# A decoder kernel on one core: order of the attention step, and the product for the values

## The reference

```
h = layernorm(x)
q, k, v = h @ Wq, src @ Wk, src @ Wv        # src is h or the context
p = softmax(scale * q k^T + mask)           # per sequence and head, 64 x 64
x = x + (p v) @ Wo
```

## Time and profile before

| | us |
|---|---|
| median of 3 runs (lowest, highest) | 4896.48 (4889.78, 4901.68) |
| the profiled execution, its own time | 4900.09 |
| its span in the profile | 4898.2 |
| mean granted TensorE clock | 0.889 |
| busy: PE, DVE, POOL, ACT | 4007.7, 3203.4, 2994.6, 2059.5 |

### The profile page before, as it was taken

How to read it: one execution, slowest core, us unless ns; L and a number is a source line. 1 busy time by engine, 2 the same in 40 slices (tenths; PEclk the granted TensorE clock), 3 DMA queues, 4 the chain that set the end, 5 groups by cost and what they waited for, 6 DMA issues and landing times. The chain is left out here.

```text
span 4898.2 us, 215645 instructions
## 1 busy us (share of the span) xinstructions
PE 4007.7 (82%) x85067; PEld 2918.6 (60%) x85076; DVE 3203.4 (65%) x10848; ACT 2059.5 (42%) x5737; POOL 2994.6 (61%) x4949
## 2 busy tenths in 40 slices
PE   8999977254899978656999997559879998889988
PEld 6777754132566666523777774335547776667766
DVE  5875668422344688787556874753337878888866
ACT  4555545011344444365555554112225543336632
POOL 6766632276455699688556762038876777777710
PEclk9999988555899998755999997879998999999999
DMA  3000012433100022200000002113431000000000
GB/s 94 5 13 19 19 28 57 78 62 54 37 0 0 18 39 39 35 1 1 2 0 15 22 18 54 42 46 75 77 62 35 0 15 16 16 9 1 0 13 24
DMA packets 380509, 139.58 MB, mean 28 GB/s; under 512 B 216487, under 2 KB 373239, under 8 KB 380055
## 3 DMA queue, kind: packets, MB, share of 16 engines
q1 hardware_dynamic: 345430, 107.60, 9.3%
q0 software_dynamic: 34816, 28.34, 4.0%
HBM read 91.46 MB, written 43.85 MB: 28 GB/s over the span
## 5 line engine op out<-in xcount | busy, mean ns | idle before, releaser
L1051 DVE TENSOR_REDUCE rowmax<-ps 128x16 f32<-128x1024 f32 x512 | 626.3, 1223 | 488.0 <-PE ps L678 487.7
L696 PE MATMUL ps<-prob,kT 32*64 32x256 f32 x9216 | 781.7, 408 | 8.7 <-issue 2.4
L721 PE MATMUL ps<-v,probT 64*64 64x64 f32 x36864 | 764.6, 227 | 5.3 <-issue 2.2
L721 PEld LDWEIGHTS ps<-v,probT 64*64 64x64 f32 x36864 | 683.8, 140 | 57.4 <-issue 16.0
L678 PE MATMUL ps<-kblock,qT 32*64 32x256 f32 x8192 | 697.0, 410 | 17.2 <-DVE rowmax L1060 14.2
L900 ACT ACTIVATE probT<-ps 128x1024 f32<-128x1024 f32 x512 | 518.0, 1012 | 353.4 <-PE ps L708 353.0
L585 POOL TENSOR_TENSOR kblock<-kT,key_scale 128x512 f32<-128x512 f32 x576 | 599.8, 1041 | 18.2 <-ACT kT L878 7.6
L587 POOL TENSOR_TENSOR prob<-qT,key_scale 128x512 f32<-128x512 f32 x576 | 601.5, 1044 | 0.0
L561 POOL TENSOR_TENSOR vareps<-moments,eps 128x1 f32<-128x1 f32 x522 | 98.8, 189 | 745.7 <-DVE negmean L1025 745.6
L887 ACT ACTIVATE xn<-x_res,nmr,rstd 128x128 f32 (+1 forms) x512 | 252.7, 494 | 513.6 <-POOL nmr L567 349.5
L708 PEld LDWEIGHTS ps<-mT,pick_bf 32*64 32x64 bf16 x16384 | 311.7, 108 | 221.2 <-ACT mT L857 74.1
(11 more groups left out here) (380 smaller groups left out, 9655.7 us busy)
## 6 DMA issues: line engine op xcount, KB each, us to landing
ctxT<-in_ctxT SPq DMA_DIRECT2D x256, 64.0 KB, 1.8
held<-in_g_w SPq DMA_DIRECT2D x16, 836.0 KB
ctxT<-in_ctxT SPq DMA_DIRECT2D x256, 32.0 KB, 1.9
table<-prob SPq DMA_DIRECT2D x32, 256.0 KB, 2.4
x_dram<-x_res SPq DMA_DIRECT2D x32, 256.0 KB, 2.4
x_res<-x_dram SPq DMA_DIRECT2D x16, 512.0 KB, 6.9
x_res<-in_x SPq DMA_DIRECT2D x8, 512.0 KB, 7.5
x_res<-in_e_w SPq DMA_DIRECT2D x64, 64.0 KB
```

The costliest lines, as they stand in the source:

```text
L696: mm = nc.tensor.matmul(out.rearrange("p (h s) -> p h s", h=GH), k.kT[rows, buf, S * b:S * b + S], k.qblock[rows, buf, :, S * b:S * b + S] ...
L721: mm = nc.tensor.matmul(k.ps_o[S * b:S * b + S, u, S * hh:S * hh + S], k.probT[rows, buf, at:at + S], k.v9[rows, buf, (HD + 1) * h:(HD + 1 ...
L1051: nc.vector.tensor_reduce(spread, heads, AX.X, ALU.max).then_inc(soft.did["max_raw"], 1)
```

## The change

PE's step now begins with queries, keys and the two transposes; then stand all the waits; then the output product, the values and the transpose of the output of it-7; then the added rows and the scores; and the mixing is last. Within the scores the maxima are subtracted first (the small products open the sum in PSUM) and the key scores are added. The values are one product of 128 columns, except in L1_xattn, which keeps two; the exchange of the halves for the last eight heads is made in the copy out of PSUM, in three instructions (all partitions and the first eight heads, and twice half the partitions and the last eight). `xnT` loses its second copy and ACT the instruction that made it (L866, and L860 in L3_ffn). ACT copies the group of `front_psum` first, then that of `yv_psum`. DVE finds the maxima first and takes the reciprocal and the normalized output last. In L3_xattn the values were one product already and their copy stays one instruction.

```diff
+WHOLE = (slice(0, P), slice(0, HEADS), slice(0, P))
+def value_parts():
+    first, second, low, high = slice(0, HEADS // 2), slice(HEADS // 2, HEADS), slice(0, S), slice(S, P)
+    return [(slice(0, P), first, slice(0, P)), (low, second, high), (high, second, low)]
...
@@ attention_pe, step
-        if value is not None or turn is not None or out is not None:
-            (the waits and products of this group)
...
+        if mixes is not None:
+            after(pe, c, "v_done", it, mb)
         after(pe, c, "kT_done", it, 3)
...
         if norm is not None:
             after(pe, c, "xn_done", it, 1)
             mm = nc.tensor.transpose(k.ps_xT, k.xn[:, b1, :], k.ident)
         if less is not None:
-            values_mixable(mixes, it, mb)
-            if early:
-                scores_writable(score1, score2, it)
             after(pe, c, "max_done", it, 5)
             mm = nc.tensor.matmul(k.ps_mT, top_halves(k.rowmax[:, b5, :]), k.ident_bf[:, :], start=True, stop=True)
         if mm is not None:
             mm.then_inc(c.front_psum, 1)
+        mm = None
+        if score1 is not None:
+            after(pe, c, "max_done", it, 4)
+            after(pe, c, "kblock_done", it, 3)
+        if score2 is not None:
+            after(pe, c, scores_read(c, it, 6), it, 6)
+            after(pe, c, "qblock_done", it, 5)
         if mixes is not None:
-            for hh in range(HEADS // 2):
-                mm = mix(mixes, (par - mb) % NB, hh)
-            mm.then_inc(mixes.did["o_psum"], 1)
+            after(pe, c, "exp_done", it, mb)
+        if value is not None or turn is not None or out is not None:
+            after(pe, c, values_read(c, it, 4), it, 4)
+            after(pe, c, "y_read", it, 9)
+            after(pe, c, "oT_done", it, 8)
+        if out is not None:
+            mm = nc.tensor.matmul(k.ps_y, k.oT[:, b8, :], weights(out, 3), start=True, stop=True)
+        if mixes is not None and turn is None:
+            after(pe, c, "on_done", it, mb + 1)
+        if value is not None:
+            source, wv = k.ctxT[:, b3, :] if value.cross else k.xnT[:, b3, :], weights(value, 2)
+            if value.name == "L1_xattn":
+                (two products, as before)
+            else:
+                mm = nc.tensor.matmul(k.ps_v, source[:, 0:P], wv, start=True, stop=True)
+        if turn is not None:
+            after(pe, c, "on_done", it, 7)
+            mm = nc.tensor.transpose(k.ps_oT, k.o[:, b7, :], k.ident)
+        if mm is not None:
+            mm.then_inc(c.yv_psum, 1)
...
         if score2 is not None:
-            mm = key_scores(score2, b5, high, first=not score2.added)
             if less is not None:
                 after(pe, c, "mT_done", it, 5)
                 for h in range(GH):
-                    mm = less_max(less, b5, h, high)
+                    less_max(less, b5, h, high)
+            mm = key_scores(score2, b5, high)
             mm.then_inc(score2.did["first_rows"], 1)
...
             after(pe, c, "first_rows", it, 5)
-            mm = key_scores(score2, b5, low, first=False)
             if less is not None:
                 for h in range(GH):
-                    mm = less_max(less, b5, h, low)
+                    less_max(less, b5, h, low)
+            mm = key_scores(score2, b5, low)
             mm.then_inc(score2.did["s2_psum"], 1)
+        if mixes is not None:
+            for hh in range(HEADS // 2):
+                mm = mix(mixes, (par - mb) % NB, hh)
+            mm.then_inc(mixes.did["o_psum"], 1)
...
@@ attention_act, step: the copies L848 and L853 move behind L878
-                    nc.scalar.activation(k.xnT[:, b1, P:P + S], k.ps_xT[:, 0:S], ACT.Copy)
...
+            for rows, heads, source in value_parts():
+                mm = nc.scalar.activation(values(k, b3)[rows, heads, :], heads_of(k.ps_v)[source, heads, :], ACT.Copy)
+            mm.then_inc(value.did["v_done"], 1)
...
@@ attention_dve, step: the block of "mixes" (L1031 to L1046) moves behind L1071
-                nc.vector.tensor_tensor(values(k, b3), heads_of(k.ps_v), heads_of(bias),
-                                        ALU.add).then_inc(value.did["v_done"], 1)
+                for rows, heads, source in value_parts() if value.softmax else [WHOLE]:
+                    mm = nc.vector.tensor_tensor(values(k, b3)[rows, heads, :], heads_of(k.ps_v)[source, heads, :],
+                                                 heads_of(bias)[source, heads, :], ALU.add)
+                mm.then_inc(value.did["v_done"], 1)
...
-        k.xnT = sb("xnT", [P, NB, P + S])
+        k.xnT = sb("xnT", [P, NB, P])
```

More of the change, by code:

```diff
@@ L688, in keys_at, with key_scores @@
         return k.s2[half:half + S, g % 2, at:at + GH * S], (32 * g, half)
-    def key_scores(part, buf, groups, first):
+    def key_scores(part, buf, groups):
         for g in groups:
@@ L698, in key_scores @@
                     k.qblock[rows, buf, :, S * b:S * b + S],
-                    start=not part.softmax or first, stop=not part.softmax, tile_position=place)
+                    start=not part.softmax, stop=not part.softmax or groups == low, tile_position=place)
         return mm
@@ L709, in less_max @@
                     out[:, S * h:S * h + S], k.pick_bf[rows, S * h:S * h + S], k.mT[rows, buf, S * b:S * b + S],
-                    start=False, stop=groups == low and h == GH - 1, tile_position=place)
+                    start=groups == high and h == 0 and not part.added, stop=False, tile_position=place)
         return mm
@@ L781, in step @@
                                   k.ctxT[:, b2, 0:P] if project.cross else k.xnT[:, b2, 0:P], start=True, stop=True)
-        early = less is None or any(part is not None and part.added for part in (score1, score2))
-        if less is None:
-            values_mixable(mixes, it, mb)
-            scores_writable(score1, score2, it)
         if norm is not None:
@@ L842, in step @@
         plain = plain if plain is not None and plain.name == "L3_xattn" else None
-        if turn is not None:
-            act.wait_ge(c.yv_psum, it - 2)
-            after(act, c, "y_read", it, 8)
-            if c.name(it, 3) in VALUE_BIAS:
-                after(act, c, values_read(c, it, 3), it, 3)
-            nc.scalar.activation(k.oT[:, b7, :], k.ps_oT, ACT.Copy).then_inc(turn.did["oT_done"], 1)
-        if value is not None and value.name not in VALUE_BIAS:
-            act.wait_ge(c.yv_psum, it - 2)
-            after(act, c, "y_read", it, 8)
-            after(act, c, "o_psum", it, 3 + NB)
-            nc.scalar.activation(values(k, b3), heads_of(k.ps_v), ACT.Copy).then_inc(value.did["v_done"], 1)
         if norm is not None or project is not None or soft is not None:
@@ L864, in step @@
             else:
-                if not norm.cross:
-                    nc.scalar.activation(k.xnT[:, b1, P:P + S], k.ps_xT[:, 0:S], ACT.Copy)
                 nc.scalar.activation(k.xnT[:, b1, 0:P], k.ps_xT, ACT.Copy).then_inc(norm.did["xT_done"], 1)
@@ L878, in step @@
                 nc.scalar.activation(k.kT[:, b2, :], k.ps_k, ACT.Copy).then_inc(project.did["kT_done"], 1)
+        if turn is not None:
+            act.wait_ge(c.yv_psum, it - 2)
+            after(act, c, "y_read", it, 8)
+            if c.name(it, 3) in VALUE_BIAS:
+                after(act, c, values_read(c, it, 3), it, 3)
+            nc.scalar.activation(k.oT[:, b7, :], k.ps_oT, ACT.Copy).then_inc(turn.did["oT_done"], 1)
+        if value is not None and value.name not in VALUE_BIAS:
+            act.wait_ge(c.yv_psum, it - 2)
+            after(act, c, "y_read", it, 8)
+            after(act, c, "o_psum", it, 3 + NB)
+            for rows, heads, source in value_parts():
+                mm = nc.scalar.activation(values(k, b3)[rows, heads, :], heads_of(k.ps_v)[source, heads, :], ACT.Copy)
+            mm.then_inc(value.did["v_done"], 1)
         if plain is not None:
@@ L1071, in step @@
                                     ALU.add).then_inc(plain.did["exp_done"], 1)
+        mixes, mb = c.mixing(it)
+        if mixes is not None and mixes.softmax:
+            inv = k.rowinv[:, :].rearrange("p (u h e) -> p u h e", u=2, e=1)
+            sums = mixed(k)[:, :, :, HD:HD + 1]
+            after(dve, c, "o_psum", it, mb)
+            if mixes.name == "L1_xattn":
+                nc.vector.tensor_scalar(inv, sums, 1e-30, None, ALU.max).then_inc(mixes.did["sum_done"], 1)
+                after(dve, c, "sum_done", it, mb)
+                nc.vector.reciprocal(k.rowinv[:, :], k.rowinv[:, :]).then_inc(mixes.did["inv_done"], 1)
+                after(dve, c, "z_stored", it, mb + NB, each=32)
+            else:
+                nc.vector.reciprocal(inv, sums).then_inc(mixes.did["inv_done"], 1)
+            after(dve, c, "inv_done", it, mb)
+            nc.vector.tensor_tensor(k.o[:, (par - mb) % NB, :].rearrange("p (u h d) -> p u h d", u=2, d=HD),
+                                    mixed(k)[:, :, :, 0:HD], inv.broadcast_to([P, 2, HEADS // 2, HD]),
```

(1 more changed line is left out.)

54 lines of the change are left out of this document (2 added, 52 removed).

## The result

The changed kernel takes 5135.02 us (median; 5131.76 to 5136.47) against 4897.55 us, a ratio of 1.0486 with a 95% interval of 1.0468 to 1.0504: 237 us slower.

A forecast was written before the change was run, and what follows sets the result against it. PE was taken as packed in L2_xattn but for a 0.23 us wait for the exponential, late through DVE, POOL and ACT. Stage terms of 2.41 us by 64 steps, 154 us, on 4900 gave 5054 us, range 4845 to 5160.

The forecast's parts named there:

- the forecast ring: The forecast's own case, subtractions held by POOL's copies in a chain through DVE and POOL: 5000 to 5100 us, chance 0.55.
- The ring in L0_attn and L2_xattn: Chain from PE through DVE and POOL and back, subtractions waiting for POOL's copies: 5.13 us a step, +0.59 each.
- PE's 0.17 and its hole are lost inside this wait: In L0_attn and L2_xattn: the single product's 0.17 us and PE's 0.23 us idle gap bring nothing.
- DVE's three value copies, 0.42, at most 0.60: In L0_xattn, L1_attn and L3_attn: DVE's copies out of PSUM take 0.42 us, at most 0.60, in place of 0.20.
- L3_attn's thin margin: First subtraction comes after copy L585 starts, by under 0.1 us, and so is caught: 5.55 us a step, +0.95.
- L3_ffn: First subtraction gets through, the second waits for L585; the exponential's chain is longer: 5.07 us a step, +0.22.
- the first rival: POOL's copies do not hold the subtractions; the exponential's chain remains, 4.47 us in L0_attn and L2_xattn: 4855 us, chance 0.14.
- L1_attn: Subtractions come past nearly all of POOL's copies and PE's own line binds: 6.10 us a step, -0.40.
- L1_xattn, taken as 0, between -0.4 and +0.87: Keeps two products and its engines' work, POOL 93 % busy: no change, between -0.4 and +0.87 us a step.
- L2_attn +0.07, L3_xattn 0: L2_attn: first subtraction just past L585's end, 5.23 us a step, +0.07; L3_xattn: chain not ending on PE, 0.
- Subtraction first, worth nothing: In the scores, maxima subtracted before the key scores: nothing, between -0.23 and +0.23 us a step.
- longer than forecast: Second subtraction in L3_ffn also meets L587 and DVE's copies cost 0.60: 5119 us; or clock falls: 5072; chance 0.16.

The follow-up runs named there:

- run 2: The changed kernel with the two subtractions replaced by memsets that read nothing, leaving out the lower two bf16 parts of the maxima: 5035.86 us.
- run 1: The changed kernel with the values by two products and one copy again, the second 64-column copy back in ACT, orders kept: 5139.68 us.
- run 8: The kernel before with the two subtractions replaced by memsets, leaving out the lower two bf16 parts of the maxima: 4817.86 us.
- run 11: The changed kernel with memsets in place of the subtractions and PE's five waits moved to just ahead of the output's transpose: 4831.55 us.
- run 6: The changed kernel with PE's five waits just ahead of the output's transpose, and DVE's reciprocal and output between reduction and subtractions: 4997.73 us.
- run 7: The kernel before with only the order within the scores changed, the maxima subtracted first: 4912.46 us.
- run 5: The changed kernel with DVE's order of before, reciprocal and output ahead of the maxima: 5675.89 us.
- run 10: The kernel before with memsets for the subtractions, the single value product where ACT copies, and ACT's order of the changed kernel: 4799.38 us.

## Why the prediction was right, and where it was not

The direction, the main mechanism and the range were right: 5054 was forecast with 4845 to 5160, 5135 came, above the 5000 to 5100 that the forecast ring itself had been given. That the range held is in part luck. The steps in the middle of the stages grew by 4.43 us in all, not by 2.41; times 64 that would be 284 us and 5184, outside the range. The forecast took every one of the 64 steps at the full rate, and the real ends of the stages lost less (247 us over the reductions) while 12 us were gained elsewhere: two things that it did not have made up for terms that it had too small. By its own steps:

- **The ring in L0_attn and L2_xattn**: right, 5.20 and 5.19 against 5.13, with L1040 at 0.6 and L1043 at 0.96 us, each ending with a copy, L1066 right behind. PE's busy share there is 85 %, as forecast. The common ends, and the memsets of run 2 that nothing holds, show that POOL's instructions cause the long subtractions. The Trainium skill, "SBUF — State Buffer", section "Who interferes with whom", names the pair: a DVE instruction with two SBUF inputs, a GpSimd instruction that reads SBUF. The trace agrees: the memsets in their place, which read nothing, took 0.07 us in mid copy. One detail was wrong: PE waits at L782 for the maxima, not at the transpose for the output. It made little difference to the sum (0.06+0.55 here, 0.03+0.58+0.08 there, 0.08 less; L989 starts 0.43 behind L794 in place of 0.36, which makes up for it), but it decided the worth of the single product (run 1).
- **"PE's 0.17 and its hole are lost inside this wait"**: wrong as to the 0.17. It is inside the ring, and in L0_attn, L2_attn, L2_xattn and L3_ffn the change would have cost that much more without it.
- **DVE's three value copies, 0.42, at most 0.60**: the term that was mis-sized, and outside its bound. From the first copy to the next instruction it is 0.72 us, and each part takes 0.22 where the whole copy took 0.28. In the timeline of L3_attn (the three copies stand in one row):

```profile
3902.73 0.68 DVE L999 TENSOR_TENSOR v<-ps,bv 128x64 f32<-128x64 f32 x3
3903.45 0.29 DVE L1018 BATCH_NORM_STATS2 stats<-x_res 128x6 f32 x1
```

  That is 0.30 more than forecast in L0_xattn (+0.35 over the forecast step) and in L3_attn (+0.37).
- **L3_attn's thin margin**: right. L1040 takes 1.008 us in the mean there, so it is caught from L585's start.
- **L3_ffn**: the mechanism was right (in 30 of 40 steps L1040 gets through at 0.18 and L1043 waits for L585, and the exponential's ring sets the step), its size was not: 5.66 against 5.07. The forecast gave 0.08 us from the exponential's end to PE; it takes 0.47; the two products take 0.55 in place of 0.45. Of that kind is the error of the first rival, too (4.47 against 5.00 in run 2: 0.43 for 0.08, 0.55 for 0.45, and 0.43 for the 0.36 from the transpose to DVE).
- **L1_attn**: 0.17 faster in place of 0.40. I had it past the copies and bound by PE's own line, by a margin of 0.01 us in my own figures (L1057 at 4.81, the end of L587, moved by DVE's copies, at 4.40+0.42), and I had left the bias L611 out of the list. It is not past them:

```profile
1454.85 0.40 DVE L1040 TENSOR_TENSOR rowmax<-rowmax 128x16 f32<-128x16 f32 x1
1455.29 0.38 DVE L1043 TENSOR_TENSOR rowmax<-rowmax 128x16 f32<-128x16 f32 x1
...
1454.18 1.04 POOL L587 TENSOR_TENSOR prob<-qT,key_scale 128x512 f32<-128x512 f32 x1
1455.18 0.46 POOL L611 TENSOR_TENSOR x_res<-x_res,bo 128x128 f32 x1
...
1455.71 0.30 PEld L782 LDWEIGHTS ps<-attn_w,oT 128*128 128x128 f32 x2 [0.18 <-DVE rowmax L1043]
```

  L1040 waits out L587 (1455.25 and 1455.22), L1043 the bias (1455.67 and 1455.64), so in all of the middle 40 steps. The hole of 0.23 that I took off PE's line is another one here, too: 0.19, a wait for the maxima (run 8). In run 11, where nothing is caught, and in run 6, where the subtractions come past the copies, the stage takes 6.13, which is what I had given to PE's line (6.10).
- **L1_xattn, taken as 0, between -0.4 and +0.87**: +0.20. One subtraction waits out L587 there, in 32 of the middle 40 steps, and without it (run 2) the step is back at 5.99.
- **L2_attn +0.07, L3_xattn 0**: +0.22 and 0. In L2_attn L1040 does come just past L585, as at 3.47 against 3.40, but then it waits out the whole of L587 (1.02 us in the median), and the step, 5.39, is a little above the 5.34 that I had as the upper end.
- **Subtraction first, worth nothing**: right in size; by itself it costs 0.3 % (run 7), a little over what I call no change.
- **The rivals**: 5135 lies nearest to "longer than forecast" (5119). Of its two parts the dearer copies came (0.72, more than its 0.60). The second catch in L3_ffn came in 10 of the middle 40 steps, L1040 behind L585 and L1043 behind L587; these steps, 5.61 us, are no longer than the others, so it cost nothing.

What stays open: what the 0.43 to 0.47 us between the exponential's end and PE's next load consist of; what divides L3_attn's excess in run 5; where the 12 us between the stages come from; and whether a kernel that takes the order of run 11 in L1_attn and L2_attn and that of run 10 elsewhere would be faster still. It wasn't tried.

## What to carry to other kernels

When two engines release each other once per step, their orders are one choice: with one of them in the new order it cost 15 and 16 % here, with both 5 %, and what counts is how much time stands in the ring from the late result to the next start. Before moving a short DVE instruction with two inputs in SBUF, lay its new time beside all of POOL's instructions, small ones as well; an instruction that is too long in the trace before (L1060 at 0.38 against 0.17) names one that the list lacks. Where such a sum hangs on a margin of 0.01 us, as in L1_attn, work out the other case too. When easing a ring, add up the next one first: here 99 and 22 us apart were 303 together.

## What the runs showed of the hardware that I had not expected

- A DVE instruction with a half or a quarter of the elements took nearly the same time: out of PSUM 128 by 64 217 ns and 64 by 64 222 ns, where 128 by 128 took 283 ns in the kernel before; and three of them hold up the next instruction for 0.72 us, one whole copy for 0.20.
- A subtraction of 128 by 16 elements waits for whichever POOL copy is running, and having been released by one it can be caught again by the next 0.03 us later; even a POOL addition of 128 by 128, 0.46 us long, holds it to its end (run 6, and L1060 in the kernel before).
- PE's busy share of 99 % is not proof that PE sets the step: L1_attn shows 99.4 % at 6.33 us, in the kernel after, and the same at 6.13 in run 11, where the maxima no longer hold L782.
